# Two small-head cross-attentions on one core: the value matmuls of a step in one run at its end, and single score blocks between the maxima

## The reference

```python
x = x + _L0_xattn_ref(ctx_1024, ctx_1024, _layernorm(x, axis=-1), L0_xattn_w_out, L0_xattn_b_out)
...
x = x + _L1_xattn_ref(_layernorm(x, axis=-1), ctx_1024, ctx_1024, L1_xattn_Wq, ...)
...
```

```python
energy = jnp.einsum('nqhd,nkhd->nhqk', q, k)
attn = jax.nn.softmax(energy / jnp.sqrt(jnp.float32(EMBED_SIZE)), axis=3)
out = jnp.einsum('nhql,nlhd->nqhd', attn, v).reshape(N, q_len, EMBED_SIZE)
return out @ w_out.T + b_out
```

## Time and profile before

| | us |
|---|---|
| median of 3 runs | 586.53 (586.2 to 589.74) |
| profiled execution | 587.63 |
| its span | 585.8 |
| PE busy in the span | 522.3 (89%) |
| DVE busy | 348.1 (59%) |
| ACT busy | 302.7 (52%) |
| POOL busy | 59.7 (10%) |
| first attention, first maximum block to last turn_out | 18.8 to 87.1 |
| second attention, the same | 177.5 to 243.0 |

### The profile page before, as it was taken

The page is one execution under the profiler, slowest core; times in us unless marked ns, Lnnn a source line. Parts: engine busy times, 40 slices in busy tenths (PEclk is TensorE's granted clock), DMA queues, the critical chain, the costliest instruction groups (busy, mean ns, idle before and its releaser), DMA issues.

```text
span 585.8 us, 8935 instructions
## 1 busy us (share of the span) xinstructions
PE 522.3 (89%) x3252; PEld 290.2 (50%) x3252; DVE 348.1 (59%) x883; ACT 302.7 (52%) x495; POOL 59.7 (10%) x151
## 2 busy tenths in 40 slices
PE   6889987999988999888978599999999959887997
PEld 2234434667832444344735235555556555544665
DVE  6777714266667885268344657777783467532654
ACT  7357772533210778427366369778782054553411
POOL 4021102000000211000073000000001220000000
PEclk9899998999998999989999899999999977998999
DMA  4669100034024200000000000000000400000000
GB/s 140 194 197 418 52 9 26 0 98 120 0 63 114 97 2 1 1 0 2 0 1 0 1 1 1 1 2 1 1 2 17 200 1 1 2 1 0 2 0 18
DMA packets 11465, 26.14 MB, mean 45 GB/s; under 512 B 2112, under 2 KB 6592, under 8 KB 10784
## 3 DMA queue, kind: packets, MB, share of 16 engines
q1 hardware_dynamic: 11424, 25.59, 13.1%
HBM read 22.44 MB, written 3.15 MB: 44 GB/s over the span
## 4 chain that ended last, share of the span: by engine, by line
PE 72%; DVE 11%; ACT 5%; issue 4%; DMA 3%; POOL 2%; SPq 2%; DVEq 0%; ACTq 0%; POOLq 0%
PE ps L1561 5%; PE ps L1572 5%; PE ps L1587 5%; PE ps L1693 5%; PE ps L1945 5%; PE ps L1684 5%; PE ps L1504 5%; PE ps L1406 4%; PE ps L1438 4%; PE ps L1954 2%; DVE mxs L855 2%; PE ps L1637 2%; PE ps L1519 2%; PE ps L1647 2%; PE ps L1624 1%
## 5 line engine op out<-in xcount | busy, mean ns | idle before, releaser
L855 DVE TENSOR_REDUCE mxs<-ps 128x1 f32<-128x512 f32 x128 | 82.3, 683 | 23.2 <-PE ps L1406 22.5
L565 ACT ACTIVATE PR<-ps 128x1024 f32<-128x1024 f32 x80 | 76.3, 972 | 25.4 <-PE ps L1448 16.2
L939 DVE TENSOR_REDUCE nm<-ps 128x1 f32<-128x512 f32 x64 | 41.1, 683 | 24.8 <-PE ps L1561 24.8
L1406 PE MATMUL ps<-Kst,Qst 84*128 84x512 bf16 x128 | 43.8, 397 | 5.9 <-DMA Qst<-q_rows 4.1
L1647 PE MATMUL ps<-ctxT,const_t 128*128 128x512 f32 x86 | 42.9, 647 | 5.9 <-DMA const_t<-in_const 5.9
L574 ACT COPY Qst<-ps 12x1024 bf16<-12x1024 bf16 x24 | 24.0, 1001 | 45.3 <-PE ps L1477 45.3
L606 ACT COPY PR<-ps 128x512 f32<-128x512 f32 x64 | 37.9, 595 | 16.8 <-PE ps L1572 16.8
L614 ACT ACTIVATE Qst<-ps,nm 128x512 f32<-128x512 f32 x64 | 45.4, 709 | 1.5 <-DVE nm L939 1.3
L1572 PEld LDWEIGHTS ps<-const_t,Qst 128*128 128x128 f32 x256 | 27.4, 140 | 24.3 <-DVE Qst L922 11.8
L1438 PE MATMUL ps<-Qst,Kst 84*128 84x256 bf16 x256 | 38.6, 273 | 0.3
L1504 PE MATMUL ps<-PR,VX 128*9 128x256 f32 x512 | 38.3, 381 | 0.0
(11 more groups left out here) (352 smaller groups left out, 848.7 us busy)
## 6 DMA issues: line engine op xcount, KB each, us to landing
Kst<-k_rows SPq DMA_DIRECT2D x48, 96.0 KB
FC<-in_fc SPq DMA_DIRECT2D x2, 2048.0 KB, 12.0
Qst<-q_rows SPq DMA_DIRECT2D x48, 48.0 KB
FC<-in_w SPq DMA_DIRECT2D x1, 2048.0 KB, 8.7
k_rows<-REP SPq DMA_DIRECT2D x12, 128.0 KB, 2.6
REP<-in_w SPq DMA_DIRECT2D x1, 1536.0 KB, 6.8
q_rows<-REP SPq DMA_DIRECT2D x20, 64.0 KB, 2.0
FC<-in_w2e SPq DMA_DIRECT2D x1, 1024.0 KB, 10.6
```

Of the source, the lines that this page charges most:

```text
L565: act.activation(PRg[:, g % 2, u * 1024:u * 1024 + width], bank(3 + 2 * (n % 2), 2)[:, 0:width], ACT.Exp, scale=scale).then_inc(s.p_ready, 1)
L855: i = dve.tensor_reduce(m[:, u // 4, u % 4:u % 4 + 1], bank(n % 2), AX_X, ALU.max)
L1406: i = pe.matmul(bank(n % 2), Qst[0:ROWS_A, b, h, q0:q0 + P], Kst[0:ROWS_A, b, h, :], start=True, stop=True)
```

## The change

Layers 0 and 1 get a loop of their own, attention_cross(a); attention(a) remains for the causal self-attention of the last stage (a = 2), which has other shapes, and loses its branches for a < 2. A step of the new loop has eight slots. Each slot holds one maximum block, then half an exponential unit: two of its four score matmuls (scores_half; the second half signals st_ready). So two maximum blocks, two fillers and a whole unit of a part become block, half, block, fillers, half. turn_max goes from behind the unit of part 2 to slot 4, between the maximum block 4 and the first half of unit 2. turn_out is in slot 1, behind unit 0 as before. All four value chunks of group s - 3 are in one run at the end of slot 7 of step s; before, the last of them was in part 0 of step s + 1. The programs of DVE, ACT, POOL and SyncE are the same, and so is the number of matmuls.

```diff
--- before.py
+++ after.py
@@ -323,6 +323,7 @@
                 stack_lots(tile)
 
         MROW0 = [0, 0, PAD]
+        PV_RUNS = {7: [0, 1, 2, 3]}
         SCALES = [float(P) ** -0.5, float(HD) ** -0.5, float(HD) ** -0.5]
 
         PAIRS3 = H // 2 * 2 * B
@@ -1391,21 +1392,12 @@
             def scores_max(a, g, part):
 
                 b, h0 = group_heads(a, g)
-                if a < 2 and part == 0:
-                    pe.wait_ge(S[f"k_loaded{b}{h0 // 4}"], 16 * NPART * (a + 1))
-                    pe.wait_ge(S[f"q_loaded{b}{h0 // 4}"], 16 * NPART * (a + 1))
-                    if a == 0:
-                        pe.wait_ge(s.sel_ready, 4 * b + h0 // 4 + 1)
                 n_banks = (MAXB[a + 1] - MAXB[a]) // G
                 for u in range(part * n_banks // 4, (part + 1) * n_banks // 4):
                     n = MAXB[a] + g * n_banks + u
                     if n >= 2:
                         pe.wait_ge(s.smax_read, n - 1)
-                    if a < 2:
-                        q0, h = (u // 4) * P, h0 + u % 4
-                        i = pe.matmul(bank(n % 2), Qst[0:ROWS_A, b, h, q0:q0 + P], Kst[0:ROWS_A, b, h, :],
-                                      start=True, stop=True)
-                    elif u == 0:
+                    if u == 0:
                         for c in range(4):
                             o = bank(n % 2)[:, c * P:(c + 1) * P]
                             pe.matmul(o, Qst[0:PAD, b, h0 + c, 0:P], K4[0:PAD, h0 // 4, b * SQ:b * SQ + P],
@@ -1430,14 +1422,7 @@
                     if n >= 2:
                         pe.wait_ge(s.p_ready, n - 1)
                     o = bank(3 + 2 * (n % 2), 2)
-                    if a < 2:
-                        h = h0 + u
-                        for k in range(4):
-                            k0 = k * P
-                            ok = o[:, k * SQ:(k + 1) * SQ]
-                            i = pe.matmul(ok, Kst[0:ROWS_A, b, h, k0:k0 + P], Qst[0:ROWS_A, b, h, :],
-                                          start=True, stop=True)
-                    elif u == 0:
+                    if u == 0:
                         for c in range(0, 4, 2):
                             ok = o[:, c * SQ:(c + 2) * SQ].rearrange("p (c q) -> p c q", c=2)
                             pe.matmul(ok, K4[0:PAD, h0 // 4, b * SQ:b * SQ + P],
@@ -1458,6 +1443,56 @@
                         i = pe.matmul(ok, identb[:, :], maskb[:, 1, :].unsqueeze(1).to_broadcast([P, 4, P]),
                                       start=False, stop=True)
                     i.then_inc(s.st_ready, 1)
+
+            def scores_half(a, g, slot):
+
+                b, h0 = group_heads(a, g)
+                u, half = slot // 2, slot % 2
+                n = UNIT[a] + 4 * g + u
+                if half == 0:
+                    pe.wait_ge(s.mrow_ready, groups(a, g) + 1)
+                    if n >= 2:
+                        pe.wait_ge(s.p_ready, n - 1)
+                for k in (2 * half, 2 * half + 1):
+                    i = pe.matmul(bank(3 + 2 * (n % 2), 2)[:, k * SQ:(k + 1) * SQ],
+                                  Kst[0:ROWS_A, b, h0 + u, k * P:(k + 1) * P], Qst[0:ROWS_A, b, h0 + u, :],
+                                  start=True, stop=True)
+                if half == 1:
+                    i.then_inc(s.st_ready, 1)
+
+            def max_block(a, g, u):
+
+                b, h0 = group_heads(a, g)
+                if u == 0:
+                    pe.wait_ge(S[f"k_loaded{b}{h0 // 4}"], 16 * NPART * (a + 1))
+                    pe.wait_ge(S[f"q_loaded{b}{h0 // 4}"], 16 * NPART * (a + 1))
+                    if a == 0:
+                        pe.wait_ge(s.sel_ready, 4 * b + h0 // 4 + 1)
+                n = MAXB[a] + g * 8 + u
+                if n >= 2:
+                    pe.wait_ge(s.smax_read, n - 1)
+                q0, h = (u // 4) * P, h0 + u % 4
+                pe.matmul(bank(n % 2), Qst[0:ROWS_A, b, h, q0:q0 + P], Kst[0:ROWS_A, b, h, :],
+                          start=True, stop=True).then_inc(s.smax_ready, 1)
+
+            def attention_cross(a):
+
+                for step in range(G + 4):
+                    for slot in range(8):
+                        if step < G:
+                            max_block(a, step, slot)
+                        if slot % 2 and step < 3:
+                            for _ in range(3 if step < 2 else 2):
+                                pe.matmul(bank(6 if step < 2 else 7), identb[:, :],
+                                          Kparts[:, 0, 0:SK] if a == 0 else onesel[:, :, :], start=True, stop=True)
+                        if slot == 4 and 0 <= step - 1 < G:
+                            turn_max(a, step - 1)
+                        if 0 <= step - 2 < G:
+                            scores_half(a, step - 2, slot)
+                        if slot == 1 and 0 <= step - 4 < G:
+                            turn_out(a, step - 4)
+                        if slot in PV_RUNS and 0 <= step - 3 < G:
+                            probs_values(a, step - 3, PV_RUNS[slot])
 
             def turn_max(a, g):
 
@@ -1525,12 +1560,6 @@
                     for part in range(4):
                         if step < G:
                             scores_max(a, step, part)
-                        if a < 2 and step < 3:
-                            for _ in range(3 if step < 2 else 2):
-                                pe.matmul(bank(6 if step < 2 else 7), identb[:, :], Kparts[:, 0, 0:SK] if a == 0 else onesel[:, :, :],
-                                          start=True, stop=True)
-                        if part == 0 and a < 2 and 0 <= step - 4 < G:
-                            probs_values(a, step - 4, [3])
                         if 0 <= step - 2 < G:
                             scores_exp(a, step - 2, part)
                         if part == 0 and 0 <= step - 4 < G:
@@ -1538,7 +1567,7 @@
                         if part == 2 and 0 <= step - 1 < G:
                             turn_max(a, step - 1)
                         if part and 0 <= step - 3 < G:
-                            probs_values(a, step - 3, ([], [0], [1], [2] if a < 2 else [2, 3])[part])
+                            probs_values(a, step - 3, ([], [0], [1], [2, 3])[part])
 
             def queries3(r):
 
@@ -1657,7 +1686,7 @@
             pe.wait_ge(s.q_split, NPART)
             pe.wait_ge(s.rows_zero, 1)
             pe.wait_ge(s.masks_ready, 1)
-            attention(0)
+            attention_cross(0)
             pe.wait_ge(s.ld_wa, 16)
             project(0, 0, WA["wo0"])
 
@@ -1744,7 +1773,7 @@
             pe.wait_ge(s.ld_zero, 16 * 4 * B)
             pe.wait_ge(s.ld_onesel, 16)
             pe.wait_ge(s.v1_read, B)
-            attention(1)
+            attention_cross(1)
             project(1, 1, WB["wo1"])
```

## The result

| | before | changed |
|---|---|---|
| median of 4 runs, us | 586.37 | 594.73 |
| ratio to before | | 1.0116, 95% interval 1.0064 to 1.0168 |
| span of the profiled execution | 585.8 | 592.4 |
| first attention, start of the first maximum matmul to start of the last turn_out | 67.8 | 72.2 |
| second attention, the same | 65.0 | 66.9 |

The table of before counted the attentions to the end of the last turn_out, some 0.4 us later.

The account below looks back on a forecast made before the run. PE bounds a full step of 6.71 us, DVE close; afterwards DVE, starved behind the long run, sets 7.31. Attentions of +2.75 and +1.65 make +4.4 us on the median 586.53: 591.0, range 586.5 to 595.

Parts of the forecast that it names:

- its two mechanisms: Full step: DVE idles 1.61 us behind the long value run, and 0.31 more as the maxima's transposes wait for its multiply.
- rival D: Inside the slots: latency from freed bank to next reduction is 0.75 us, not 0.53; 596 us, chance 0.20 (with ACT's cover failing).
- The full step: Steps 4 to 7 of the cross-attentions: DVE sets 7.31 us, +0.60 over the 6.71 of before.
- The drains: PE in a full step: four value runs become one, saving 3 x 0.22 = 0.66 us of entry and exit.
- PE's floor of 6.25: PE's own work in a full step: 6.71 - 0.66 for value runs + 0.2 for transposes standing alone = 6.25 us.
- PE busy 6.2 to 6.4: Profile after, full step: PE busy 6.2 to 6.4 us of 7.2 to 7.4, no longer all of it.
- rival B: Full steps: the drain gain arrives, DVE doesn't starve and PE's 6.25 us holds; -4.6 us, 582, chance 0.08.
- The o_ready wait: Slot 4: turn_max waits for DVE's multiply with block 5 queued behind it; 0.31 us more idle DVE a full step.
- rival C: Full steps: only the long run's wait remains, the wait for DVE's multiply is hidden; 588.5 us, chance 0.17.
- The second attention: Second cross-attention: +2.45 us from step 3 on, less 0.8 for an earlier start of step 3, so +1.65.
- The first attention: First cross-attention: +2.45 us from step 3 on, plus 0.3 for a later start of step 3, so +2.75.
- Step 3 starts 0.3 later: First attention: block 5 queued behind turn_max's wait for GpSimd in step 1 costs 0.9 us, of which step 2 returns 0.6.

Follow-up runs that it names:

- e5: Changed kernel, but DVE reduces only the first 256 of 512 columns of each maximum block in the two changed attentions: ratio 0.9898, full step 6.37 us.
- e1: Kernel before with all four value chunks of a group in one run at the end of part 3, order otherwise unchanged: ratio 1.0071, full step 7.04 us.
- e2: Changed kernel with the maxima's transposes in slot 5 instead of slot 4: ratio 0.9989, full step 6.82 us.

## Why the prediction was right

Forecast: +4.4 us, 591.0, by way of DVE; measured some +6.8 by the ratio and +6.3 in the two attentions of the traces. The direction, the new bound and its two mechanisms held; the sum was short in one place. The median, 594.73, lies inside the whole range (586.5 to 595) but over the 589.5 to 593 of this forecast alone: it is the room left for rival D that holds it, and D didn't occur.

- **The full step.** 7.31 forecast, 7.32 measured. That it fits to 0.01 is luck: the terms were off and cancelled. A pair of reductions shows 1.29 us because the row holds the tail of the last one; when the next block is ready they start 0.60 apart (1.89 = 2 x 0.60 + 0.69), so eight take 4.8 and not 5.16. In return the wait behind the run was 1.74 and not 1.61, and from start to start it costs 1.82 (2.42 from the last reduction before it to the first behind it, less 0.60); one part of this is that behind values a reduction starts 0.50 after its matmul (55.40 to 55.90), not 0.42. And the wait at the multiply costs 0.48 from start to start (the reductions of 58.50 and 59.58 are 1.08 apart), not 0.31. Together 4.8 + 0.2 + 1.82 + 0.48 = 7.3.
- **The drains.** 1.85 us for the run of 32 and 0.43 behind it: right, and hidden, as said. PE's floor of 6.25 was worked out from 6.71 as if PE had no wait in it. It had some 0.15 (matmuls that start at 62.74 and 63.06 and the like), and e5, with 0.26 of waiting in 6.37, shows a need of some 6.1. The sign "PE busy 6.2 to 6.4" failed too, 6.67, since the modelled ends cover PE's short waits for DVE. Nothing in the sum hung on it. What rival B would give is what e5 shows.
- **The o_ready wait** (rival C was its absence) is the larger half of the step's loss, 0.50; the long run costs 0.33, and the spread of the blocks gives 0.22 back. The forecast had them equal, 0.30 for the run with the spread (measured 0.11) and 0.31 for the wait.
- **The second attention**: +1.65 forecast, +1.9 measured. From step 4 to the end it is +2.0 as forecast (+2.05): among this step 9, where the sums' copy comes 4.59 us behind the first of the exponentials (4.58 forecast; 4.26 before). Up to step 4 the forecast was -0.4 and the measurement -0.1: step 3 starts 0.6 earlier, not 0.8, and loses 0.5 of it, not 0.4. Step 9:

```profile
242.67 3.77 ACT L566 ACTIVATE PR<-ps 128x1024 f32<-128x1024 f32 x4
...
247.26 0.37 ACT L583 COPY scr<-ps 128x256 f32<-128x256 f32 x1 [0.82 <-PE ps L1539]
```

- **The first attention**: +2.75 forecast, +4.4 measured. From step 4 on it is +2.1, again as forecast; up to there +2.35, where +0.7 was forecast. This is the step that failed in size: "Step 3 starts 0.3 later"; from the first maximum block it starts 1.9 later (22.6 against 20.7 us). Block 5 behind the wait costs 0.9, though step 2 was to return 0.6 of it, and a clock of 1.00 was taken for the blocks behind it, from rows of steps 8 and 9, whose gaps of PE are short. Here PE waited 3.55 us in one piece, and the fall to 0.50 cost 2.7. The context landed 1.3 earlier in that execution, and GpSimd finished as much earlier, which hid part of it.
- **Rival D** (the margin inside the slots is missing) did not occur: behind a long run three reductions in a row start 0.60 apart, and no step has idle time at every reduction.

## What to carry to other kernels

Before batching matmuls to save drains, take the consumer's stock of work (here two banks, 1.29 us) and compare it with the length of the run (1.85 us) plus the matmul in front and behind: a run longer than the stock starves the consumer, and that is only free when the consumer has that much slack. When work is moved ahead in an in-order queue, look up each of its waits and what stands behind it; one slot was worth 0.5 us a step. And when a change makes a wait of the tensor engine longer, look at the granted clock behind it: the fall cost 2.7 us here, three times what the order of blocks cost. One profile isn't enough for that, since where the clock is low differs from one execution to the next.

## What the runs showed of the hardware

- A run of value matmuls (9 output rows) between matmuls of 128 output rows costs 0.10 us going in and 0.12 to 0.13 coming out, whatever its length: runs of 8, 16 and 32 take 0.55, 0.98 and 1.85 us.
- The fourteen traces hold 32 single waits of PE of 3.16 to 6.01 us after the first 10 us (the four in step 1 named above, and in later stages of each kernel one of 3.9 and one of 3.7). In or shortly behind every one of them the granted clock was 0.50, for several us.
- Shorter waits went both ways. In step 1 those of 0.41 to 2.29 us left it at 1.00 but for e1. At the start of the second attention those of 1.82 (e2) to 3.00 us (e1) were followed by 0.50 in all fourteen traces (the kernel before: 2.66, low from 177.7 to 181.1). So the length of one wait alone doesn't tell it.
- Reductions of 128 x 512 from PSUM on DVE start 0.60 to 0.61 apart when the next block is ready, though each shows 0.68 to 0.69. A timeline row of several can hold short idle times: one of eight in steps 0 and 1 of the kernel before shows 5.18 us and holds one of 0.10, with starts 0.61 to 0.78 apart.
